# Talking-heads attention with a 64-key cut between two feed-forward blocks: sign and distance arrays awaited by their last reader only, a tie verdict in five POOL operations, value products in quarters

## The chip, the cores and the metric

The kernel runs on one core of one Trainium2 chip. Its engines are PE (TensorE, matrix products), DVE (VectorE), ACT (ScalarE), POOL (GpSimd) and SP (SyncE, which issues the DMA transfers). The metric is the device time of one launch in microseconds, the median of several runs. The profile and the trace come from one further, profiled execution.

## The reference

Input `x` is 4 batches of 1024 tokens with 256 features, all in float32. Two half-weight feed-forward blocks with ternary weights stand around an attention, each behind a layer norm:

```python
x = x + 0.5 * ffn(_layernorm(x))
x = x + attn(_layernorm(x))
x = x + 0.5 * ffn(_layernorm(x))
```

The attention has 16 heads of width 64 and 4 memory keys ahead of the 1024 keys. What sets the work around the change is this part:

```python
dots = jnp.einsum('bhid,bhjd->bhij', l2norm(q), l2norm(k)) * 10.0
dots = jnp.einsum('hg,bgij->bhij', W_pre_th, dots)
dots = jnp.where(causal, mask_value, dots)
vk = jax.lax.top_k(dots, 64)[0][..., -1:]
dots = jnp.where(dots < vk, mask_value, dots)
attn = jnp.einsum('hg,bgij->bhij', W_post_th, softmax(dots))
out = jnp.einsum('bhij,bhjd->bhid', attn, v)
```

Then `out` is scaled by head, multiplied by a sigmoid gate and projected by `Wo`.

## The kernel before

It has three parts. `first_stage` does the first feed-forward block and the projections to queries, keys, values and gates, which it stores in HBM. `attention` does the attention. `last_stage` does the second feed-forward block. The change lies in `attention` alone.

**Tiles.** A *block* is 128 tokens of a batch (`G`, 32 of them; `ib = G % 8` is its place in the batch). A block has 16 *groups* `g` of 8 tokens; with the 16 heads a group is a tile of 128 rows (head and token) by as many keys as the last token sees, 4 + 8·(t + 1) of them, so rows grow from 12 to 1028 within a batch. Two groups are a *pair* `p`, and the loop of every engine runs over pairs: `for k in range(S + 16)` with `S = 256`. In iteration `k` each engine works at several pairs at once, in stages. The order on each engine is written out by hand; engines meet by semaphores only.

**Life of a pair.** PE's `units` multiply queries and keys for the *next* block (L873, L874) into two banks, DVE's `scored` copies them to `Sn` (L1197), SP stores them (L787) and loads them back by group as `Sg` (L797). `mix` (L887) mixes heads; DVE's `take` (L1208) writes the result to `D`. The mixed scores are negated, so the cut keeps the smallest. The 64th is found by search: ACT's `count(g, r)` (L1002) counts signs against a guess `nt`, rounds `r` 0 to 3, and POOL's `better` (L1086, L1087, L1090) makes the next guess. Round 3 leaves the signs as the int8 array `SG`. POOL's `nearest` computes the count that is off (`off`), its sign (`sgn`), and the array of scaled distances `W` (L1103), and `pos`. DVE's `sides` (L1223, semaphore `near`) joins `SG` and `W`; `closest` (L1231, `best`) takes the 8 largest, `m8`; `picked` (L1239, `pick`) picks the one at place `pos`, and L1243 (`vk`) turns it into the threshold. POOL's `judge` (L1110 to L1116) writes `bad`, which is not zero where the 64th was not among the eight or where there is a tie; PE's `missed` (L900, L901) adds `bad` up inside `mix`, DVE copies the sum to `flag` (L1204) and branches on it in `threshold`. `select` (L1287, `prob`) cuts the exponentials `E`, `inverse` (L1294) inverts their sums, POOL's `spread` (L1122) scales the second mixing matrix, PE's `post` (L914) mixes, and ACT's `turned` (L1025, L1030) copies the result to `AT`.

**Value products.** When half a block (`hb`, 64 of them, one every 4 iterations) is in `AT`, PE's `values(hb, part_)` multiplies it with `V` (L934, L940) for 8 pairs of heads. Half of the pairs are done in iteration `k = 4 hb + 8`, behind `units(G, slots[1])`, and half at the start of the next iteration. The first part waits for `AT`, and in an even half also for `V` (`v_in`), which SP's `late` loads in iteration 7 of 8 (L804, L805). At the end the semaphore `av` lets DVE's `gated` (L1300) and ACT's next `turned` go on. `units` come in four `slots` per iteration, in the first six iterations of a block; each `units` call waits for DVE's copy of the one before (`s_sb`).

**POOL's order in iteration k:** `better(k-2, 3)`, `judge(k-3)`, `better(k-1, 1)`, `nearest(k-2)`, `better(k-1, 2)`, `spread` twice, `first(k)`. A `chain` around an operation makes the next one wait for it.

Of the kernel before, what the change touches and what calls it, by code (L numbers as in the profile page):

```python
# [11 lines left out]
P = 128  # L12
# [24 lines left out]
ALU = mybir.AluOpType  # L37
# [570 lines left out]
NB = B * IB  # L608
# [61 lines left out]
def attention(nc, banks, mkT, qd, kd, gd, vd, x1d, x2d, sd, mix_rows, mem_v, Wo_d, delta_c,  # L670
# [34 lines left out]
    with ExitStack() as ctx:  # L705
        def sb(name, shape, dt=F32):
            return ctx.enter_context(nc.sbuf_tensor(name, shape, dt))
# [42 lines left out]
        pick = sb("pick", [P, 8])  # L750
        vk = sb("vk", [P, 8])
        tie = sb("tie", [P, 4, 8])
        far = sb("far", [P, 8])
        bad = sb("bad", [P, 8], BF16)
        onesb = sb("onesb", [P, 1], BF16)
        deltab = sb("deltab", [R8, P], BF16)
# [105 lines left out]
        def _(pe):  # L862
# [55 lines left out]
            def values(hb, part_):  # L918
                G, ib = hb // 2, hb // 2 % IB
                if part_ == 0:  # L920
                    pe.wait_ge(s["at"], PC[8 * (hb + 1)])
                    if hb == 0:
                        pe.wait_ge(s["w_in"], 32)
                    if hb % 2 == 0:
                        pe.wait_ge(s["v_in"][G % 2], 32 * (G // 2 + 1))
                        if G >= 1:
                            pe.wait_ge(s["x_ok"], G)
                    if hb >= 1:
                        pe.wait_ge(s["ut"], hb)
                for p in range(4 * part_, 4 * part_ + 4):  # L930
                    for c in range(ib + 1):
                        for h in (2 * p, 2 * p + 1):
                            lo = DH * (h % 2)
                            out = nc.tensor.matmul(ps[7][lo:lo + DH, p * DH:(p + 1) * DH],  # L934
                                                   V[:, c, h * DH:(h + 1) * DH], AT[:, c, h, :], start=(c == 0),
                                                   stop=(c == ib and (ib > 0 or hb % 2 == 0)))
                        if c == 0 and hb % 2 == 1:
                            for h in (2 * p, 2 * p + 1):
                                lo = DH * (h % 2)
                                out = nc.tensor.matmul(ps[7][lo:lo + DH, (p + 1) * DH - R8:(p + 1) * DH],  # L940
                                                       V[0:MEM, ib + 1, h * DH:(h + 1) * DH], ATt[:, h, :],
                                                       start=False, stop=(ib == 0))
                if part_ == 1:
                    out.then_inc(s["av"], 1)

            def project(G):
# [9 lines left out]
            for k in range(S + 16):  # L956
                G = k // 8 + 1
                held = (k - 5) % 4 == 0
                slots = [range(0)] * 4
                if G < NB and k % 8 < UNITS // 4:  # L960
                    slots = unit_slots(G)[4 * (k % 8):4 * (k % 8) + 4]
                if k >= 9 and (k - 9) % 4 == 0 and (k - 9) // 4 < 2 * NB:
                    values((k - 9) // 4, 1)
                if k < S:
                    mix(2 * k, k - 3)
                if 0 <= k - 5 < S and not held:
                    post(2 * (k - 5) + 1)
                units(G, slots[0])
                if 0 <= k - 5 < S and held:
                    post(2 * (k - 5) + 1)  # L970
                if k < S:
                    mix(2 * k + 1, k - 3)
                elif searched(k - 3):
                    if k == S:
                        pe.wait_ge(s["taken"], TC[NT])
                    else:
                        pe.wait_ge(s["flag"], FP[k - 3])
                    missed(k - 3, ps[2]).then_inc(s["mixed"], 1)
                units(G, slots[1])
                if k >= 8 and (k - 8) % 4 == 0 and (k - 8) // 4 < 2 * NB:  # L980
                    values((k - 8) // 4, 0)
                if k >= 14 and (k - 14) % 8 == 0 and (k - 14) // 8 < NB:
                    project((k - 14) // 8)
                units(G, slots[2])
                if 0 <= k - 4 < S:
                    post(2 * (k - 4))
                units(G, slots[3])

        @block.scalar
        def _(act):  # L990
            def count(g, r):
                e, n, i = g % 8, reach(g), 2 * FP[g // 2] + g % 2
                act.wait_ge(s[f"nt{r}"], FP[g // 2] + 1)
                if r == 3:
                    if i >= 2:
                        act.wait_ge(s["pick"], i - 1)
                    out = SG[:, g % 2, 0:n]
                else:
                    if r == 0 and i >= 2:
                        act.wait_ge(s["cnt2"], i - 1)  # L1000
                    out = junk[:, g % 2, 0:n]
                nc.scalar.activation(out, D[:, e, 1:1 + n], ACT.Sign, bias=nt[:, r, e:e + 1], scale=-1.0,  # L1002
                                     accum_out=cnt[:, r, e:e + 1]).then_inc(s[f"cnt{r}"], 1)
# [57 lines left out]
        def _(pool):  # L1061
            links = [0]

            def chain(ins):
                links[0] += 1
                ins.then_inc(s["chain"], 1)
                pool.wait_ge(s["chain"], links[0])
# [24 lines left out]
            def nearest(p):  # L1092
                e, t = cells(p)
                pool.wait_ge(s["cnt3"], 2 * FP[p] + 2)
                chain(tt(off[:, e], tab[:, XN, t], cnt[:, 3, e], ALU.subtract))
                ts(sgn[:, e], off[:, e], -1.0, 1.0, ALU.max, ALU.min).then_inc(s["side"], 1)
                pool.wait_ge(s["side"], FP[p] + 1)
                pool.wait_ge(s["prob"], 2 * p - 2)
                for g in (2 * p, 2 * p + 1):
                    n, i = reach(g), 2 * FP[p] + g % 2  # L1100
                    if i >= 2:
                        pool.wait_ge(s["pick"], i - 1)
                    ts(W[:, g % 2, 0:n], D[:, g % 8, 1:1 + n], sgn[:, g % 8:g % 8 + 1], -SMALL, ALU.mult,  # L1103
                       ALU.mult).then_inc(s["v"], 1)
                tt(pos[:, e], off[:, e], sgn[:, e], ALU.mult).then_inc(s["pos"], 1)

            def judge(p):
                e, t = cells(p)
                pool.wait_ge(s["pos"], FP[p] + 1)
                chain(tt(tie[:, 0, e], nt[:, 3, e], sgn[:, e], ALU.mult))  # L1110
                chain(ts(tie[:, 1, e], tie[:, 0, e], SMALL, None, ALU.mult))
                ts(far[:, e], pos[:, e], 15.5, None, ALU.is_gt)
                pool.wait_ge(s["pick"], 2 * FP[p] + 2)
                chain(tt(tie[:, 2, e], m8[:, e, 0], tie[:, 1, e], ALU.add))
                chain(ts(tie[:, 3, e], tie[:, 2, e], 0.0, None, ALU.is_equal))
                tt(bad[:, e], tie[:, 3, e], far[:, e], ALU.add).then_inc(s["bad"], 1)  # L1116

            def spread(g):
                pool.wait_ge(s["rinv"], g // 2 + 1)
# [535 lines left out]
```

## Time and profile before

| | |
|---|---|
| median of 3 runs | 3963.88 us (3955.75 to 3964.03) |
| profiled execution | 3937.97 us, span on the core 3936.2 us |
| mean granted TensorE clock | 0.925 |
| PE busy | 3343.1 us (85%) |
| DVE busy | 2941.1 us (75%) |
| ACT busy | 2526.4 us (64%) |
| POOL busy | 2040.2 us (52%) |
| DMA | 466.45 MB, mean 119 GB/s |

Busy time of PE counts matmuls whose ends are modelled, so a busy PE is not one at its peak. A granted clock of 1.00 is 2.4 GHz, of 0.50 it is 1.2 GHz. The attention runs from about 996 to 3640 us of the span; the shares above average it with the two feed-forward parts. The idle time of an engine that nobody waits for costs nothing.

### The profile page before, as it was taken

The page shows a single profiled execution, that of the slowest core. Times are in us where ns is not written, and L with a number is a line of the kernel's source. Part 1 is how long each engine was busy: PE and PEld are TensorE (multiplying, and loading weights), DVE is VectorE, ACT ScalarE, POOL GpSimd, SP SyncE. Part 2 cuts the span into 40 slices and gives each one's busy share as a digit, 9 for nine tenths or more (in the row PEclk, how much of TensorE's full clock was granted, in tenths as well). Part 3 has the DMA queues.
Part 4 walks back from the last instruction along what each step waited for, and adds up shares of the span by engine and source line. Part 5 has one row for each costly group of instructions (what it writes and reads, how often), then busy time and mean ns, then how long its engine had stood idle before and what let it go on. Part 6 is the DMA issues. An engine that isn't in the chain of part 4 may idle for free. (4 is left out here: it accounts for less than half of the span.)

```text
span 3936.2 us, 72868 instructions
## 1 busy us (share of the span) xinstructions
PE 3343.1 (85%) x22950; PEld 2129.3 (54%) x22950; DVE 2941.1 (75%) x6619; ACT 2526.4 (64%) x5825; POOL 2040.2 (52%) x5777
## 2 busy tenths in 40 slices
PE   7999999995788888878888857888888888888798
PEld 4444444442455556645555644555566555566566
DVE  6778887775578888668888876888885788877254
ACT  2433443332587889768888936788895788888221
POOL 1221111222676667577666727766675776666232
PEclk9999999997699999989999977999998899999899
DMA  3222222223455654345555414555643455642110
GB/s 127 81 81 80 96 86 80 79 82 124 126 157 158 171 162 120 80 135 168 164 167 161 97 41 137 160 162 168 172 95 95 140 160 167 173 124 52 53 33 27
DMA packets 362423, 466.45 MB, mean 119 GB/s; under 512 B 29525, under 2 KB 294101, under 8 KB 361561
## 3 DMA queue, kind: packets, MB, share of 16 engines
q1 hardware_dynamic: 361944, 461.02, 40.0%
q8 instruction: 185, 3.03, 0.4%
q14 instruction: 294, 2.40, 0.2%
HBM read 226.57 MB, written 234.36 MB: 117 GB/s over the span
## 5 line engine op out<-in xcount | busy, mean ns | idle before, releaser
L1002 ACT ACTIVATE junk<-D,nt 128x76 int8<-128x76 f32 (+62 forms) x1440 | 1070.5, 746 | 178.6 <-POOL nt L1087 142.9
L914 PE MATMUL banks<-kr,E 128*128 128x128 f32 (+1 forms) x4672 | 732.4, 307 | 194.1 <-issue 96.2
L914 PEld LDWEIGHTS banks<-kr,E 128*128 128x128 f32 (+1 forms) x4672 | 627.4, 210 | 302.6 <-issue 279.1
L887 PE MATMUL banks<-Sg,kpre 128*128 128x109 f32 (+51 forms) x1568 | 647.1, 513 | 19.5 <-DVE D L1208 9.4
L873 PE MATMUL banks<-kT,qT 64*128 64x343 f32 (+11 forms) x896 | 399.6, 529 | 184.7 <-DVE Sn L1197 163.3
L1025 ACT ACTIVATE AT<-banks 128x512 f32<-128x512 f32 (+3 forms) x768 | 344.9, 478 | 324.0 <-PE banks L934 166.6
L1287 DVE SCALAR_TENSOR_TENSOR E<-D,vk,E 128x12 f32<-128x12 f32 (+56 forms) x512 | 378.4, 757 | 212.3 <-DVE vk L1243 136.0
L1223 DVE SCALAR_TENSOR_TENSOR W<-SG,sgn,W 128x76 f32<-128x76 int8 (+14 forms) x480 | 413.3, 900 | 82.9 <-POOL W L1103 80.7
L1197 DVE COPY Sn<-banks 128x686 f32<-128x686 f32 (+7 forms) x448 | 376.7, 841 | 129.9 <-PE banks L874 116.6
L523 DVE RECIPROCAL a_share<-a_share 128x512 f32<-128x512 f32 x128 | 429.2, 3353 | 4.4
L934 PE MATMUL banks<-AT,V 128*64 128x64 f32 x9216 | 367.4, 232 | 59.6 <-issue 43.4
L1002 ACT ACTIVATE SG<-D,nt 128x76 int8<-128x76 f32 (+14 forms) x480 | 356.6, 746 | 67.5 <-DVE hit L1239 65.0
L1103 POOL TENSOR_SCALAR W<-D,sgn 128x76 f32<-128x76 f32 (+14 forms) x480 | 343.2, 725 | 109.4 <-issue 72.7
L874 PE MATMUL banks<-kT,qT 64*128 64x343 f32 (+11 forms) x896 | 399.8, 529 | 0.0
L1208 DVE TENSOR_SCALAR_CACHE_REDUCE D<-banks 128x13 f32<-128x13 f32 (+62 forms) x504 | 340.1, 675 | 55.2 <-PE banks L891 54.6
L934 PEld LDWEIGHTS banks<-AT,V 128*64 128x64 f32 x9216 | 314.1, 143 | 115.1 <-issue 91.6
L1086 POOL TENSOR_TENSOR move<-cnt,tab 128x2 f32<-128x2 f32 x720 | 257.1, 357 | 210.1 <-ACT junk L1002 206.8
L887 PEld LDWEIGHTS banks<-Sg,kpre 128*128 128x128 f32 x1568 | 275.6, 210 | 149.0 <-issue 109.8
L1012 ACT ACTIVATE E<-D,least 128x12 f32<-128x12 f32 (+56 forms) x512 | 343.6, 720 | 18.3 <-DVE D L1208 16.0
L467 POOL TENSOR_TENSOR a_g2T<-a_gT 128x512 f32<-128x512 f32 x64 | 72.4, 1135 | 542.7 <-ACT a_gT L385 542.6
L1231 DVE MAX8 m<-W 128x8 f32<-128x76 f32 (+14 forms) x480 | 324.5, 712 | 0.0
L295 PE MATMUL banks<-a_xbT,a_W 128*128 128x512 f32 x512 | 248.2, 610 | 50.0 <-DVE a_share L527 49.1
(187 smaller groups left out, 5537.3 us busy)
## 6 DMA issues: line engine op xcount, KB each, us to landing
score_scratch<-Sn SPq DMA_DIRECT2D x96, 343.0 KB, 3.3
q_scratch<-a_share SPq DMA_DIRECT2D x32, 512.0 KB, 2.7
v_scratch<-a_share SPq DMA_DIRECT2D x32, 512.0 KB, 3.7
k_scratch<-a_share SPq DMA_DIRECT2D x32, 512.0 KB, 2.8
gate_scratch<-a_share SPq DMA_DIRECT2D x32, 512.0 KB, 2.8
kT<-k_scratch SPq DMA_DIRECT2D x32, 512.0 KB, 4.7
qT<-q_scratch SPq DMA_DIRECT2D x32, 512.0 KB, 6.3
gateT<-gate_scratch SPq DMA_DIRECT2D x32, 512.0 KB, 11.8
```

What stands on the lines that cost most here:

```text
L523: link(nc.vector.reciprocal(ri[:, c % 2, :], rr[:, c % 2, :]))
L873: nc.tensor.matmul(ps[0][:, 0:c1 - c0], qT[0:DH, p, :], kT[0:DH, p, c0:c1], start=True, stop=True)
L874: nc.tensor.matmul(ps[1][:, 0:c1 - c0], qT[DH:P, p, :], kT[DH:P, p, c0:c1], start=True, stop=True).then_inc(s["s_ps"], 1)
L887: out = nc.tensor.matmul(bank[:, 0:c], kpre[:].rearrange("p h r -> p (h r)"), Sg[:, g % 3, c0:c1], start=True, stop=not diagonal)
L914: out = nc.tensor.matmul(ps[5 + i % 2][0:rows, c % 4 * P:(c % 4 + 1) * P], E[:, g % 4, c * P:c * P + rows], kr[:, g % 4, :], start=True, s ...
L934: out = nc.tensor.matmul(ps[7][lo:lo + DH, p * DH:(p + 1) * DH], V[:, c, h * DH:(h + 1) * DH], AT[:, c, h, :], start=(c == 0), stop=(c == ...
L1002: nc.scalar.activation(out, D[:, e, 1:1 + n], ACT.Sign, bias=nt[:, r, e:e + 1], scale=-1.0, accum_out=cnt[:, r, e:e + 1]).then_inc(s[f"cnt ...
L1012: nc.scalar.activation(E[:, g % 4, 0:n], D[:, e, 1:1 + n], ACT.Exp, bias=least[:, e:e + 1], scale=-1.0).then_inc(s["exp"], 1)
L1025: out = nc.scalar.activation(AT[:, c0:c0 + c, :, t * R8:(t + 1) * R8], bank[:, 0:c * P].rearrange("p (c h r) -> p c h r", h=H, r=R8), ACT. ...
L1197: nc.vector.tensor_copy(Sn[:, i % 2, :, 0:c1 - c0], banks[:, 0:2, 0:c1 - c0]).then_inc(s["s_sb"], 1)
L1223: nc.vector.scalar_tensor_tensor(out=W[:, h, 0:n], in0=SG[:, h, 0:n], scalar=sgn[:, e:e + 1], in1=W[:, h, 0:n], op0=ALU.is_equal, op1=ALU. ...
L1287: nc.vector.scalar_tensor_tensor(out=E[:, g % 4, 0:n], in0=D[:, g % 8, 1:1 + n], scalar=vk[:, g % 8:g % 8 + 1], in1=E[:, g % 4, 0:n], op0= ...
```

## The change

ACT's third `count` waits for `near` (DVE has read `SG`) in place of `pick`. POOL's `nearest` waits for `best` (DVE has read `W`) in place of `pick`. `judge` drops the array `far`: a pick that found nothing leaves `vk` at zero, so the verdict is now whether the product of `vk` and the tie sum is zero. It has five operations, the third waits for `best`, the fourth for `vk`. `values` works in four parts of two pairs of heads: part 0 ahead of `units(G, slots[1])`, part 1 behind it, parts 2 and 3 at the start of the next iteration.

```diff
@@ attention
-        far = sb("far", [P, 8])
@@ values
-                for p in range(4 * part_, 4 * part_ + 4):
+                for p in range(2 * part_, 2 * part_ + 2):
...
-                if part_ == 1:
+                if part_ == 3:
                     out.then_inc(s["av"], 1)
@@ the loop on PE
                 if k >= 9 and (k - 9) % 4 == 0 and (k - 9) // 4 < 2 * NB:
-                    values((k - 9) // 4, 1)
+                    values((k - 9) // 4, 2)
+                    values((k - 9) // 4, 3)
...
+                if k >= 8 and (k - 8) % 4 == 0 and (k - 8) // 4 < 2 * NB:
+                    values((k - 8) // 4, 0)
                 units(G, slots[1])
                 if k >= 8 and (k - 8) % 4 == 0 and (k - 8) // 4 < 2 * NB:
-                    values((k - 8) // 4, 0)
+                    values((k - 8) // 4, 1)
@@ count
                 if r == 3:
                     if i >= 2:
-                        act.wait_ge(s["pick"], i - 1)
+                        act.wait_ge(s["near"], i - 1)
@@ nearest
                     if i >= 2:
-                        pool.wait_ge(s["pick"], i - 1)
+                        pool.wait_ge(s["best"], i - 1)
@@ judge
-                pool.wait_ge(s["pos"], FP[p] + 1)
+                pool.wait_ge(s["side"], FP[p] + 1)
                 chain(tt(tie[:, 0, e], nt[:, 3, e], sgn[:, e], ALU.mult))
                 chain(ts(tie[:, 1, e], tie[:, 0, e], SMALL, None, ALU.mult))
-                ts(far[:, e], pos[:, e], 15.5, None, ALU.is_gt)
-                pool.wait_ge(s["pick"], 2 * FP[p] + 2)
+                pool.wait_ge(s["best"], 2 * FP[p] + 2)
                 chain(tt(tie[:, 2, e], m8[:, e, 0], tie[:, 1, e], ALU.add))
-                chain(ts(tie[:, 3, e], tie[:, 2, e], 0.0, None, ALU.is_equal))
-                tt(bad[:, e], tie[:, 3, e], far[:, e], ALU.add).then_inc(s["bad"], 1)
+                pool.wait_ge(s["vk"], FP[p] + 1)
+                chain(tt(tie[:, 3, e], tie[:, 2, e], vk[:, e], ALU.mult))
+                ts(bad[:, e], tie[:, 3, e], 0.0, None, ALU.is_equal).then_inc(s["bad"], 1)
```

PE's order in iteration 16, where the value products of the second block begin, first before the change (each row is an instruction, its tiles and the semaphores that it waits for; lines of the changed kernel are lower by one):

```order
1100 L900 MATMUL banks<-bad,onesb 1x1 [waits t_bad0]
1101 L901 MATMUL banks<-bad,onesb 1x1
1102 L873 MATMUL banks<-kT,qT 128x258 [waits t_kmean0,t_s_sb0,t_q_in0,t_k_in1]
1103 L874 MATMUL banks<-kT,qT 128x258
1104 L934 MATMUL banks<-AT,V 64x64 [waits t_x_ok0,t_ut0,t_v_in1,t_at0]
1105 L934 MATMUL banks<-AT,V 64x64 x15
1106 L873 MATMUL banks<-kT,qT 128x259 [waits t_s_sb0]
1107 L874 MATMUL banks<-kT,qT 128x259
```

and in the changed kernel:

```order
1101 L899 MATMUL banks<-bad,onesb 1x1 [waits t_bad0]
1102 L900 MATMUL banks<-bad,onesb 1x1
1103 L933 MATMUL banks<-AT,V 64x64 [waits t_x_ok0,t_ut0,t_v_in1,t_at0]
1104 L933 MATMUL banks<-AT,V 64x64 x7
1105 L872 MATMUL banks<-kT,qT 128x258 [waits t_kmean0,t_s_sb0,t_q_in0,t_k_in1]
1106 L873 MATMUL banks<-kT,qT 128x258
1107 L933 MATMUL banks<-AT,V 64x64 x8
1108 L872 MATMUL banks<-kT,qT 128x259 [waits t_s_sb0]
1109 L873 MATMUL banks<-kT,qT 128x259
```

The score product of 128x258 has moved behind eight of the sixteen value products, and so behind their four waits. On POOL, `judge` before the change:

```order
232 L1110 TENSOR_TENSOR tie<-nt,sgn 128x2 [waits t_pos0]
233 L1111 TENSOR_SCALAR tie<-tie 128x2 [waits t_chain0]
234 L1112 TENSOR_SCALAR far<-pos 128x2 [waits t_chain0]
235 L1114 TENSOR_TENSOR tie<-m,tie 128x2 [waits t_pick0]
236 L1115 TENSOR_SCALAR tie<-tie 128x2 [waits t_chain0]
237 L1116 TENSOR_TENSOR bad<-tie,far 128x2 [waits t_chain0]
```

and in the changed kernel:

```order
226 L1112 TENSOR_TENSOR tie<-nt,sgn 128x2 [waits t_side0]
227 L1113 TENSOR_SCALAR tie<-tie 128x2 [waits t_chain0]
228 L1115 TENSOR_TENSOR tie<-m,tie 128x2 [waits t_best0,t_chain0]
229 L1117 TENSOR_TENSOR tie<-tie,vk 128x2 [waits t_vk0,t_chain0]
230 L1118 TENSOR_SCALAR bad<-tie 128x2 [waits t_chain0]
```

One instruction is gone, and two of the five wait for two semaphores.

## Rows read from the trace of the kernel before

**Rows 1.** By stretch: us, busy PE, PEld, DVE, ACT, POOL, clock, DMA share, GB/s.

```profile
996.00:3640.00 2644.00, 2221.50 (x19354) 1522.28 (x19354) 2061.48 (x5407) 2087.07 (x5143) 1774.56 (x5564) 0.91 0.50 138
```

**Rows 2.** Waits of PE, attention stage: us in total, times, longest us.

```profile
PE banks L934 <- issue: 43.4, 18, 4.3
```

**Rows 3.** Timeline, PE: start, us, engine, line, tiles, [idle before <-releaser]; an opening.

```profile
1015.50 0.98 PE L873 MATMUL banks<-kT,qT 64*128 64x389 f32 x1
...
1016.28 0.85 PE L873 MATMUL banks<-kT,qT 64*128 64x389 f32 x1
...
1021.65 1.12 PE L934 MATMUL banks<-AT,V 128*64 128x64 f32 x16 [4.48 <-DMA V<-v_scratch]
```

**Rows 4.** Timeline, PE: the opening one block later.

```profile
1073.86 0.48 PE L873 MATMUL banks<-kT,qT 64*128 64x258 f32 x1
...
1077.84 1.97 PE L934 MATMUL banks<-AT,V 128*64 128x64 f32 x32 [3.28 <-issue]
1079.74 0.80 PE L873 MATMUL banks<-kT,qT 64*128 64x259 f32 x1
...
1080.34 0.63 PE L873 MATMUL banks<-kT,qT 64*128 64x259 f32 x1
```

**Rows 5.** Timeline, PE: openings with longer rows, in the third batch.

```profile
2493.41 2.50 PE L934 MATMUL banks<-AT,V 128*64 128x64 f32 x48 [1.55 <-issue]
...
2566.68 2.08 PE L934 MATMUL banks<-AT,V 128*64 128x64 f32 x64 [2.16 <-issue]
2568.70 0.59 PE L873 MATMUL banks<-kT,qT 64*128 64x387 f32 x1
```

**Rows 6.** Timeline, DVE: copies of scores at the opening of rows 4.

```profile
1075.76 0.68 DVE L1197 COPY Sn<-banks 128x516 f32<-128x516 f32 x1
...
1081.09 0.70 DVE L1197 COPY Sn<-banks 128x518 f32<-128x518 f32 x1 [4.03 <-PE banks L874]
```

**Rows 7.** Timeline, ACT: the same opening.

```profile
1082.02 0.51 ACT L1002 ACTIVATE SG<-D,nt 128x252 int8<-128x252 f32 x1 [4.02 <-DVE hit L1239]
...
1084.08 0.38 ACT L1025 ACTIVATE AT<-banks 128x256 f32<-128x256 f32 x1 [0.96 <-PE banks L934]
```

**Rows 8.** Waits of all engines, attention stage.

```profile
ACT junk L1002 <- POOL nt L1087: 142.9, 223, 2.0
...
DVE W L1223 <- POOL W L1103: 80.7, 74, 2.2
DVE gateT L1300 <- PE banks L934: 79.7, 38, 9.8
...
ACT SG L1002 <- DVE hit L1239: 65.0, 34, 4.5
```

**Rows 9.** Timeline, DVE: a second half of a block.

```profile
2608.36 0.95 DVE L1197 COPY Sn<-banks 128x774 f32<-128x774 f32 x1
...
2616.75 0.69 DVE L1300 TENSOR_TENSOR gateT<-banks,gateT 128x512 f32<-128x512 f32 x1 [1.53 <-PE banks L934]
```

**Rows 10.** Busy time by stretch: iteration of rows 9, then behind the waits of rows 4 and 5.

```profile
2606.70:2616.70 10.00, 10.00 (x181) 7.94 (x179) 6.97 (x19) 4.27 (x12) 5.24 (x19) 1.00 0.39 126
1077.90:1084.00 6.10, 6.10 (x73) 4.98 (x73) 2.13 (x11) 1.20 (x6) 1.73 (x8) 0.50 0.28 82
2566.70:2572.00 5.30, 5.30 (x122) 4.56 (x124) 2.62 (x9) 2.75 (x9) 1.74 (x9) 1.00 0.34 118
```

**Rows 11.** Timeline, POOL: judge and nearest in an iteration of short rows.

```profile
2402.49 0.23 POOL L1111 TENSOR_SCALAR tie<-tie 128x2 f32<-128x2 f32 x1
2402.80 0.22 POOL L1112 TENSOR_SCALAR far<-pos 128x2 f32<-128x2 f32 x1
2403.08 0.22 POOL L1114 TENSOR_TENSOR tie<-m,tie 128x2 f32<-128x2 f32 x1
...
2404.81 0.23 POOL L1096 TENSOR_SCALAR sgn<-off 128x2 f32<-128x2 f32 x1
2405.14 0.83 POOL L1103 TENSOR_SCALAR W<-D,sgn 128x188 f32<-128x188 f32 x2
```

## The prediction

> **What bounds the kernel now.** I read the busy time by stage first, then the list of waits, then single stretches of the timeline. In the attention stage [rows 1] no engine is saturated: PE is busy 2221.50 of 2644.00 us, ACT 2087.07, DVE 2061.48, POOL 1774.56. The stage is bounded by whichever chain ends last in each of its 256 iterations, so each edit has to be priced where it stands.
>
> The edits touch two kinds of place. The first is the iteration in which a block's value products begin: every eighth one, called here an *opening*. The attention part has 32. The list of PE's waits [rows 2] shows that value products (L934) wait 43.4 us in 18 places for something the trace does not name. What it is shows in the one place beside these that has a name, in [rows 3]: PE has finished the score product of `units(G, slots[1])` (L873, from 1015.50, ends 1017.1) and then stands 4.48 us, until 1021.65, for the DMA into `V`. [rows 4] show the same picture one block on, now labelled "issue": the score product is done at 1074.6, the value products start at 1077.84 after 3.28 us. The second opening of [rows 5] waits 1.55 us, the third 2.16. Everybody else stands too: DVE's next copy of scores (L1197) has waited 4.03 us for PE [rows 6], ACT's `count(...,3)` 4.02 us for DVE's pick [rows 7]. So whatever PE does *after* `V` has landed is the critical path of all engines, and what it does *before* is free.
>
> The second place is POOL's `judge`, six small operations once per pair, ahead of `better(k-1, 1)`, for which ACT waits (L1087: 142.9 us in 223 places), and ahead of `nearest`, for which DVE waits (L1103: 80.7 us in 74 places) [rows 8].
>
> **Value products in quarters.** Nothing is added or removed; `units(G, slots[1])`, its copy on DVE and its store on SP go behind the first quarter. At the second opening of a batch the two lists of PE's order show this: the L934 row with the wait for `t_v_in` stood behind the two rows of 128x258, and stands ahead of them now. PE is in order, so the wait for `V` now holds the score product as well.
>
> Cost at an opening that waits. The score product was hidden in the wait; now it lies behind it. In [rows 3] it takes 1.6 us (two rounds, 0.98 and 0.85, starting 0.78 apart). In [rows 4] it ran at 0.48 us a matmul before the wait; behind the wait the clock is lower, and its twin there (128x259) takes 0.80 and 0.63, in all 1.23 us from 1079.74 to 1080.97. I take 1.2. Behind the wait of 2.16 us the twin's matmul takes 0.59 us against 0.80 [rows 5], so all of it 1.23 × 0.59 / 0.80 = 0.9 us; I take that, and for the opening of 1.55 us, which lies between, 1.1. Then `units(G, slots[2])` waits for the copy of `slots[1]`, which now runs beside the second quarter only: a copy of 0.68 us [rows 6] beside 1.0 us of products fits; with the longer rows the copy is near 1.0 us (0.95 in [rows 9]) and the quarter, half of 2.08 us [rows 5], just equals it, so I add 0.1 us. Four batches give 4 × 1.6 = 6.4, 4 × 1.2 = 4.8, 4 × 1.2 = 4.8 and 4 × 1.0 = 4.0 us, 20 in all. That is 16 openings; of the 16 others I take every third to wait as well, 5 × 1.0 us, since the 18 places are two more than 16 and short waits go under other names. Sum: **25 us later**. All engines stand there, so nothing hides it. Behind the moved copy stand two `MAX8`, the pick and, on SP, the store and the next load of `Sg`; they shift with PE. Bounds: 10 us (only the 18 waits, half a us each) to 34 us (every product at the low rate).
>
> Cost at the other half-blocks (iterations 4 of 8): PE is busy 10.00 of the 10.00 us from the moved score product to the end of the value products [rows 10], so the order of its work is neutral for it. The copy on DVE that started at 2608.36 comes later by at most a quarter's products less what DVE still had to do, about 1.1 us, and DVE then stands 1.53 us before the gating product anyway [rows 9]; over the stage it stands there 79.7 us in 38 places [rows 8], 2.1 us each: 0 us. Were it gone, 20 such iterations would cost some 10 us. Nor is there a gain: the intent could only be that PE fills a gap ahead of `units(G, slots[1])`, and in [rows 4] that product has no idle time before it.
>
> The clock. After the 3.28 us wait PE's granted clock is 0.50 (1.2 GHz) over the next 6.10 us; after the one of 2.16 us it is 1.00 (2.4 GHz) [rows 10]. The waits of the 8 openings of the 1.55 and 2.16 us kind grow by the 0.8 to 0.9 us that the score product filled, to 2.4 and 3.1 us, towards the length after which the clock was low. A stretch of 6 us at half rate gives away 3 us. Bounds 0 and 8 × 3 = 24 us; nearest are the rows of 2.16 us, full rate, so I take one stretch, **3 us**.
>
> The Trainium skill, "TensorE: Matmul & The Clock Gate", section on HAM oscillation, says that a PE which repeatedly waits for a DMA falls back to the low clock at each wait, and that the cost is half of the throttled time. It speaks against this change, since the waits grow; by it all 8 stretches would turn slow, 24 us in place of my 3, and the sum would be 37. The rows agree for the long wait only [rows 10].
>
> **The verdict in five operations.** `far` goes, 240 times. From the start of `far` to the start of the next operation is 0.28 us; from the one before it to `far` 0.31 [rows 11]. Two of the remaining five now wait for two semaphores; the nearest such row is L1103, which waits for three and starts 0.33 us behind L1096, 0.02 to 0.05 above a chained one. Net 0.28 − 2 × 0.02 = 0.24 us less per pair. It counts where POOL is the chain itself. Both DVE and ACT wait for POOL in the iterations of the short rows; DVE does so in 74 places [rows 8], of which some 24 lie just ahead of an opening's wait and are swallowed by it. 50 × 0.24 = **12 us earlier**. Bounds: 0, and 223 × 0.24 = 53 us, if every wait of ACT for L1087 passed it on. I stay near the 50, since in the long rows those waits go back to DVE's pick.
>
> Where `judge` waits for DVE, `m8` is there early and the last thing is now `vk`, 0.2 us after the pick, with two operations behind it in place of three: equal within 0.1 us, 0.
>
> **Earlier releases.** ACT's `count(...,3)` waits for `near` in place of `pick`: 65.0 us in 34 places go [rows 8]. But right behind it ACT stands again, for the value products: in [rows 7] 0.96 us after the two counts. ACT would reach that wait 4 us earlier and leave it at the same time. POOL's `nearest` waits for `best`, but `judge`, ahead of it on the same engine, waits for more. Both 0 us; bounds 0 and, if ACT's two counts of some 0.5 us were the chain in all 34, 34 us earlier.
>
> **Sum** against the profiled execution of 3937.97 us: +25 + 3 − 12 = +16 us, so 3954. The median of the runs is 3963.88, 26 us above that execution, and the measured time will be of that kind: 3964 + 16 = **3980 us**.
>
> **Rivals.**
> (a) *POOL is the bound and the change wins.* Each pair is one lap from `cnt` through `better`, `judge`, `nearest` back to `cnt`; a lap shorter by 0.24 us shortens the stage wherever ACT waits for L1087. For it: 223 such places. Against: in the openings everything stands for `V`, and in long rows POOL itself waits for DVE's pick. Price: −53 + 25 = −28 us, 3936. It decides from about 117 of the 223 laps on (28 / 0.24). Chance 0.15.
> (b) *The two edits balance.* Half of the moved score product is regained because engines that stood longer at an opening find their buffers free later. +13 − 12 = about +1, 3965. For it: PE waits 2 to 3 us again in the two iterations that follow each opening. Against: those waits are for DVE, which is late by the same amount. Chance 0.25.
> (c) *The clock rule holds in full*: 25 + 24 − 12 = +37, 4001. Chance 0.10; the row at 2.16 us is against it.
> (d) *The reordering is hidden*: the wait for `V` shrinks because its DMA is issued no later while the engines arrive later. Against: the load is issued in the iteration before, ahead of anything moved. It falls under (b).
> My forecast has 0.50.
>
> **How the numbers follow.** Unmistakable is a difference of over 0.2%, 8 us, about what a measurement of this kernel tells from none. Slower: most of the forecast (0.46), of (b) 0.02, and (c) 0.10: 0.58. Same: 0.04 of the forecast, 0.17 of (b), 0.02 of (a): 0.23. Faster: 0.13 of (a) and 0.06 of (b): 0.19. The range leaves out the far end of (a) and the top of (c): −12 to +36 us, 3952 to 4000. The forecast alone would be 3970 to 3992.
>
> **What would show it.** In the changed profile the wait of L933 at the openings must be longer by 0.7 to 1.6 us, its sum near 60 instead of 43.4, with DVE's and ACT's standing as long; the score product of 128x258 must stand behind it. The idle time before ACT's SG must be near zero and that before AT larger by as much. `judge` must take 1.37 us in place of 1.61 from first to last start. The iterations of the short rows between two openings must be shorter by 0.2 us each. I am wrong if an opening, from the last product before `V` to the next `mix`, is not longer by a microsecond, or if the iterations in between win more than 0.3 us each.

## The result, and the profile after

The changed kernel takes 4000.52 us (median of 6 runs, 3989.25 to 4008.64), the kernel before 3958.76 us on the same chip (6 runs, 3951.72 to 3964.03). The ratio is 1.010 with a 95% interval of 1.008 to 1.0121: **42 us slower**. The sign of the prediction held (3980 us); the result lies half a microsecond above the top of its range (3952 to 4000), and the size did not hold: +42 in place of +16.

The profiled executions differ by more than the medians: 4008.64 us after (the slowest of its six) and 3937.97 before (below all six). Sums over the two traces therefore overstate the loss by some two thirds, and I read them for places rather than for sizes.

The attention stage of the changed kernel, in the columns of [rows 1]:

```profile
996.00:3712.00 2716.00, 2270.66 (x19362) 1549.76 (x19363) 2062.95 (x5397) 2084.00 (x5141) 1716.68 (x5320) 0.89 0.48 134
```

All of the difference lies here, 72 us; the stages ahead of and behind it keep their lengths. DVE and ACT are busy as long as before, POOL 58 us less (the verdict's operation is gone), PE 49 us more with 8 instructions more recorded, at a granted clock of 0.89 in place of 0.91: the same matmuls, slower.

Waits of the changed kernel, attention stage (us in total, times, longest), of PE, ACT, DVE and POOL, to be held against [rows 2] and [rows 8]:

```profile
PE banks L933 <- issue: 70.1, 20, 6.7
PE banks L933 <- DMA V<-v_scratch: 13.0, 2, 7.0
...
ACT AT L1027 <- PE banks L933: 298.1, 59, 9.0
ACT junk L1004 <- POOL nt L1089: 130.9, 193, 2.1
ACT SG L1004 <- POOL nt L1089: 2.4, 4, 0.6
...
DVE Sn L1199 <- PE banks L873: 187.0, 130, 7.2
DVE gateT L1302 <- PE banks L933: 72.1, 35, 9.7
DVE W L1225 <- POOL W L1105: 72.1, 69, 2.1
```

The value products' wait is up from 43.4 to 70.1 us (with the openings in which the trace names the DMA, from 47.9 to 83.1), and DVE's wait for score products from 105.2 to 187.0. ACT no longer waits for the pick (65.0 us then, 2.4 from another source now), and stands for the value products instead: 298.1 us, where the kernel before has 166.6. The two lines of the kernel before:

```profile
DVE Sn L1197 <- PE banks L874: 105.2, 90, 4.5
```

```profile
ACT AT L1025 <- PE banks L934: 166.6, 55, 9.0
```

One opening shows what a microsecond of order turned into. It is the second of [rows 5], at iteration k = 160, where the value products of the fourth block of the third batch begin. PE in the changed kernel:

```profile
2606.74 1.98 PE L933 MATMUL banks<-AT,V 128*64 128x64 f32 x32 [3.45 <-issue]
...
2608.65 1.01 PE L873 MATMUL banks<-kT,qT 64*128 64x386 f32 x1
...
2609.46 0.85 PE L873 MATMUL banks<-kT,qT 64*128 64x386 f32 x1
2610.23 1.97 PE L933 MATMUL banks<-AT,V 128*64 128x64 f32 x32
...
2612.14 0.64 PE L873 MATMUL banks<-kT,qT 64*128 64x387 f32 x1
...
2616.14 1.18 PE L886 MATMUL banks<-Sg,kpre 128*128 128x271 f32 x4
```

and the granted clock there (columns as in [rows 1]):

```profile
2606.70:2612.00 5.30, 5.26 (x68) 4.10 (x68) 1.58 (x3) 2.30 (x8) 0.38 (x2) 0.50 0.10 31
```

In the kernel before, the mix that follows that opening starts at

```profile
2572.65 1.18 PE L887 MATMUL banks<-Sg,kpre 128*128 128x271 f32 x4
```

From the first value product to that mix the kernel before took 2572.65 − 2566.68 = 5.97 us, all of it at 2.4 GHz [rows 10]; the changed one takes 2616.14 − 2606.74 = 9.40. The score product that has moved behind the wait is 0.85 us of the 3.43 (its twin in [rows 5] takes that, from 2568.70 to the next operation at 2569.55). The rest is the clock: the wait is 3.45 us where it was 2.16, PE's clock behind it is 0.50, and what would take 2.02 + 0.85 = 2.87 us lasts from 2606.74 to 2612.14, 5.40 us: 2.5 us more.

One pair of executions cannot say, though, that the change made the clock fall at this opening. `judge_only` below has the old order of PE, and in its profiled execution the same opening went like this:

```profile
2572.28 3.68 PE L933 MATMUL banks<-AT,V 128*64 128x64 f32 x64 [2.72 <-issue]
...
2580.94 1.18 PE L886 MATMUL banks<-Sg,kpre 128*128 128x271 f32 x4
```

with this clock behind the wait (columns as in [rows 1]):

```profile
2572.30:2577.60 5.30, 5.30 (x69) 4.10 (x69) 0.40 (x1) 0.99 (x4) 0.66 (x4) 0.50 0.28 97
```

2580.94 − 2572.28 = 8.66 us with the old order at the low clock, 9.40 with the new one: 0.74 us for the order, and 2.7 us for a low clock that comes with either order. What can be counted is how often it comes. I took the granted clock of the 6 us behind the first value product of each of the 32 openings, in one profiled execution per kernel. Below 0.80 it is in 11, 13, 15, 12 and 12 openings with the old order there (the kernel before, `q_undone`, `judge_only`, `rel_only`, `ahead_odd`) and in 20, 20, 22, 17 and 24 with the new one (the changed kernel, `q_only`, `ahead_open`, `q_rel`, `q_judge`): eight more on average.

### The profile page after: what moved, and what is told of

It is laid out like the page before. It is cut to its first block and busy times, and to the rows that moved or that the text cites. A ratio compares the mean times of both kernels' runs of the same rounds, so it can differ in the third digit from the quotient of the medians.

```text
span 4006.9 us, 73108 instructions
## 1 busy us (share of the span) xinstructions
PE 3391.1 (85%) x22950; PEld 2155.8 (54%) x22950; DVE 2943.9 (73%) x6619; ACT 2523.5 (63%) x5825; POOL 1983.0 (49%) x5537
## 5 line engine op out<-in xcount | busy, mean ns | idle before, releaser
L913 PE MATMUL banks<-kr,E 128*128 128x128 f32 (+1 forms) x4672 | 741.2, 309 | 185.2 <-issue 86.9
L1027 ACT ACTIVATE AT<-banks 128x512 f32<-128x512 f32 (+3 forms) x768 | 346.3, 480 | 473.5 <-PE banks L933 298.1
L872 PE MATMUL banks<-kT,qT 64*128 64x343 f32 (+11 forms) x896 | 421.2, 554 | 177.9 <-DVE Sn L1199 156.1
L933 PE MATMUL banks<-AT,V 128*64 128x64 f32 x9216 | 387.9, 236 | 99.0 <-issue 70.1
L873 PE MATMUL banks<-kT,qT 64*128 64x343 f32 (+11 forms) x896 | 421.2, 554 | 0.0
L933 PEld LDWEIGHTS banks<-AT,V 128*64 128x64 f32 x9216 | 326.6, 146 | 162.5 <-issue 135.2
```

Source lines behind the costliest of these rows:

```text
L872: nc.tensor.matmul(ps[0][:, 0:c1 - c0], qT[0:DH, p, :], kT[0:DH, p, c0:c1], start=True, stop=True)
L873: nc.tensor.matmul(ps[1][:, 0:c1 - c0], qT[DH:P, p, :], kT[DH:P, p, c0:c1], start=True, stop=True).then_inc(s["s_ps"], 1)
L913: out = nc.tensor.matmul(ps[5 + i % 2][0:rows, c % 4 * P:(c % 4 + 1) * P], E[:, g % 4, c * P:c * P + rows], kr[:, g % 4, :], start=True, s ...
L1027: out = nc.scalar.activation(AT[:, c0:c0 + c, :, t * R8:(t + 1) * R8], bank[:, 0:c * P].rearrange("p (c h r) -> p c h r", h=H, r=R8), ACT. ...
```

## The experiments

There were twelve runs in three groups, with the quarters, the verdict and the releases taken apart first. Each ratio is against the kernel before on the same chip; 0.001 is 4 us.

**Each part alone.** `q_only` is the kernel before with the quarters and no other edit; shown is the new order, the new size of a part is left out:

```diff
+                if k >= 8 and (k - 8) % 4 == 0 and (k - 8) // 4 < 2 * NB:
+                    values((k - 8) // 4, 0)
                 units(G, slots[1])
                 if k >= 8 and (k - 8) % 4 == 0 and (k - 8) // 4 < 2 * NB:
-                    values((k - 8) // 4, 0)
+                    values((k - 8) // 4, 1)
```

> The kernel before with the quarters alone; verdict and releases as before. Theory A (the score product behind the wait for V, plus the low clock that follows, is the whole loss): slower than before by 45 to 60 us, a little more than the change itself (42 us), since the shorter verdict is missing. Theory B (the loss comes from the new waits in the verdict or the releases): within 10 us of before.

`q_undone` is the changed kernel with this edit taken back, so the verdict and the releases together.

> The changed kernel with the value products in halves as before, so verdict in five operations and earlier releases alone. Theory A: 5 to 12 us faster than before (0.24 us in some 30 to 50 laps of POOL). Theory B: slower than before by 20 us or more. If the shorter lap is swallowed by the wait for V: within 3 us of before.

`judge_only` has only the new `judge`, `rel_only` only the two lines `act.wait_ge(s["near"], i - 1)` and `pool.wait_ge(s["best"], i - 1)`.

> The kernel before with the verdict in five operations alone. All of the gain of the two small edits should be here: 5 to 12 us faster than before. If waiting for vk instead of pick costs something in the iterations in which DVE is late, 0 to 5 us slower.

> The kernel before with the earlier releases alone (near for the signs, best for the distances). My reading: no change, within 4 us of before, with ACT's wait for the pick (65 us) gone and its wait for the value products longer by as much. Rival: ACT's two counts were the chain, then 10 to 34 us faster.

| kernel | median us | ratio | 95% |
|---|---|---|---|
| q_only | 4017.02 | 1.0177 | 1.0159 to 1.0194 |
| q_undone | 3950.40 | 0.9997 | 0.9983 to 1.0012 |
| judge_only | 3953.73 | 1.0011 | 0.9997 to 1.0025 |
| rel_only | 3950.89 | 0.9997 | 0.9984 to 1.0009 |

The whole loss is the quarters'. Alone they cost 1.77%, 70 us (65 by the difference of the medians), more than the change as a whole. The verdict and the releases are worth nothing that these runs can tell without the quarters. The verdict's missing gain is seen in the wait for `V`. PE in `judge_only`:

```profile
PE banks L933 <- issue: 53.9, 19, 5.1
```

and in `q_undone`:

```profile
PE banks L933 <- issue: 56.0, 19, 4.9
```

against the 43.4 of [rows 2]. The iterations ahead of an opening do get shorter by 0.27 us each, in some 18 places (from one `rinv` of DVE to the next, in both traces), 5 us in all, and PE then stands longer at the openings: 53.9 and 56.0 us in place of 47.9 (43.4, and the 4.48 of [rows 3]).

That these waits are for `V`, though the trace calls them "issue", can be read off SP. From its second transfer into `V` (L805) to the first value product it takes, as means of the first five blocks of a batch, 10.2 to 10.9 us in the kernel before, 10.3 to 11.3 in `q_undone` and 10.3 to 11.1 in the changed kernel, whatever PE does meanwhile.

**Which half-blocks.** Both kernels are the changed one, with the first quarter ahead of `units(G, slots[1])` in only some iterations: for `ahead_open` in iterations 0 of 8, the openings, for `ahead_odd` in iterations 4 of 8.

```diff
+                due = k >= 8 and (k - 8) % 4 == 0 and (k - 8) // 4 < 2 * NB
+                ahead = k % 8 == 4
+                if due and ahead:
+                    values((k - 8) // 4, 0)
                 units(G, slots[1])
+                if due and not ahead:
+                    values((k - 8) // 4, 0)
+                if due:
+                    values((k - 8) // 4, 1)
```

> The changed kernel, but the first quarter goes ahead of the score product only in the openings (iteration 0 of 8, where the wait for V stands); in iteration 4 of 8 both quarters come behind it. If only the openings cost: as slow as the change, 38 to 45 us over before. If iteration 4 costs too (its period grew by 0.6 to 1.4 us in the profile): 25 to 35 us over before.

> The complement: the first quarter ahead of the score product only in iteration 4 of 8, where PE had no gap. If only the openings cost: 5 to 10 us faster than before, like the kernel without quarters. If iteration 4 costs too: 5 to 15 us slower than that one.

`ahead_open` 3996.86 us, ratio 1.0106 (1.008 to 1.0132); `ahead_odd` 3954.35 us, 1.0002 (0.9986 to 1.0018). The loss comes from the 32 openings alone; behind a block's middle the same reordering is free, to within 7 us. Nor do all openings pay: in the sixth and seventh block PE does not wait for `V`, and in six of these eight openings the iteration is at most 0.15 us longer (15.65 and 15.21 us in `ahead_open`, from one pair of `bad` products to the next, in place of 15.51 and 15.06 in `q_undone`); the other two are longer by 0.7 to 0.8.

**How much of it is the clock.** `warm_after` keeps the changed order and gives PE products of 128x128 to do, into the bank that the value products overwrite, before it waits for `V`:

```diff
+                    if hb % 2 == 0 and hb >= 2:
+                        for _ in range(WARM.get(ib, 0)):
+                            nc.tensor.matmul(ps[7][:, 0:P], ...)
```

with `WARM = {0: 18, 1: 16, 2: 8, 3: 8, 4: 6}` by block of the batch.

> The changed kernel with 6 to 18 idle products of a constant into the bank of the value products ahead of the wait for V, in the openings of the first five blocks of a batch. They read and write nothing that is used. If the low clock behind the longer wait is more than half of the loss: 20 to 35 us faster than the change, and the score product behind the wait takes 0.7 to 1.0 us instead of 1.2 to 1.9. If the loss is the order alone: within 5 us of the change.

3986.52 us, ratio 1.0085 (1.0062 to 1.0108). That is 35 us over the kernel before on the same chip, where the changed kernel is 42 over and `ahead_open` 45: a gain of 6 to 10 us, with intervals that overlap, and below what I expected. (The 14 us between this median and the changed kernel's 4000.52 are no measure: the kernel before is 7 us faster, too, beside the one than beside the other.) PE at the opening of [rows 4] in this kernel (L927 are the fillers, each recorded as two):

```profile
1075.99 4.55 PE L927 MATMUL banks<-kpre 128*128 128x128 f32 x32
1080.57 0.69 PE L938 MATMUL banks<-AT,V 128*64 128x64 f32 x16
1081.18 0.48 PE L873 MATMUL banks<-kT,qT 64*128 64x258 f32 x1
```

The quarter takes 0.69 us here. In the changed kernel it takes 1.12, behind a wait of 6.66 us:

```profile
1081.28 1.12 PE L933 MATMUL banks<-AT,V 128*64 128x64 f32 x16 [6.66 <-issue]
1082.33 0.79 PE L872 MATMUL banks<-kT,qT 64*128 64x258 f32 x1
```

So the clock is kept here, and 35 us of the loss remain. It is kept at most openings, not at all: the low clock comes in 7 of the 32, among them three of the third blocks, where PE waits another 1.83 to 3.91 us behind too few fillers and then reads 0.72 or 0.73. A second reading agrees in size. Over the 29 runs of the kernel before that stand beside the first group, a mean granted clock lower by 0.001 goes with 2.1 us more. Its mean clock there is 0.9197, that of the changed kernel's six runs, taken at another time, 0.9152: 4.5 × 2.1 = 9 us. A third is an estimate of what it can be at most: 6 us times one less the clock, summed over the 32 openings, is 24 to 32 us in the five kernels with the old order and 39 to 57 in the five with the new one, 19 us more on average, if all of it lies on the path. The clock thus accounts for 6 to 19 us of 42; where in between is not shown.

**The other way round: an earlier load.** If what stands behind `V`'s landing is the path, an earlier landing should win. `early_v` is the kernel before with the two transfers into `V` issued at k % 8 == 6, ahead of the next block's keys and queries, and taken out of `late`:

```diff
+                if k % 8 == 6 and G < NB:
+                    fetch(G)
                 if k % 8 == 6 and G + 2 < NB:
                     keys(G + 2)
                     queries(G + 2)
```

> The kernel before with the load of V issued one iteration earlier (6 of 8), ahead of the keys and queries of the next block but one. If the openings are bound by that load: the waits of the value products in the openings of the first five blocks go (about 45 us of idle time), and the kernel is 30 to 60 us faster than before. If something else is late next (the pick, the probabilities): 0 to 15 us faster.

3999.61 us, ratio 1.0121 (1.0094 to 1.0149): **48 us slower**, where 30 to 60 us faster were expected. The wait for `V` is gone from PE's list, and this has come in its place:

```profile
PE banks L892 <- DMA Sg<-score_scratch: 77.4, 23, 6.0
```

Issues of this kernel, KB each, median us to landing:

```profile
kT<-k_scratch SPq DMA_DIRECT2D x32, 512.0 KB, 12.2
qT<-q_scratch SPq DMA_DIRECT2D x32, 512.0 KB, 14.1
```

and of the kernel before:

```profile
kT<-k_scratch SPq DMA_DIRECT2D x32, 512.0 KB, 4.7
qT<-q_scratch SPq DMA_DIRECT2D x32, 512.0 KB, 6.3
```

Three transfers of some 500 KB now run together, and the `Sg` load that SP issues behind them, which the next `mix` needs, comes late. The Trainium skill, "DMA: Bandwidth & Descriptors", section "Queues, rings and completion order", says that on each DMA engine a queue's descriptors are taken in ring order; these rows agree with it: what is issued behind `V` on SP pays for `V`. Transfers that only share the bandwidth would look the same, and SP itself is held up, too: it spends 7.04 us on issuing the `Sg` load at 1068.40. Which of these it is was not tested. The load's place in the kernel before was the better one of the two.

**Verdict and releases on top of the quarters.** The quarters alone cost 70 us, the whole change 42. Which of the other two gives back the difference? `q_rel` is `q_only` with the releases, `q_judge` is `q_only` with the verdict.

> The kernel before with the quarters and the two earlier releases (near, best), and the old verdict on POOL. Quarters alone were +65 to 70 us against before, all three edits +42; so the other two give back about 25 us once the quarters are in, although each was worth 0 alone. Theory one (the releases do it: with the quarters DVE's pick comes late behind the wait for V, and ACT's SG count and POOL's nearest, which waited for the pick, stood in the chain): this kernel comes out near +42 to +48. Rival (the shorter verdict does it, since POOL's laps are the chain in the delayed iterations behind an opening): this kernel stays near +65 to +70. Half each: near +55.

> The kernel before with the quarters and the new five-operation verdict, which waits for vk and side, and the old releases. The theory that the releases alone give back the 25 us expects +63 to +70 against before; the rival, that the shorter verdict does, expects +42 to +48; half each: near +55. Outside the first stage of each iteration nothing else differs from the run with the quarters alone.

`q_rel` 4008.74 us, ratio 1.0148 (1.0121 to 1.0174); `q_judge` 4012.22 us, 1.0146 (1.0123 to 1.0169). Against 1.0177 each gives back some 12 us; neither theory of "it alone" holds, and half each, the third case, does. The intervals overlap that of `q_only`, which ran on another chip, so 12 is a best value and no more. Where the releases get it shows in ACT's waits. `q_only`:

```profile
ACT AT L1028 <- PE banks L934: 142.5, 53, 9.0
ACT SG L1005 <- DVE hit L1242: 141.6, 47, 6.4
```

`q_rel`:

```profile
ACT AT L1028 <- PE banks L934: 275.1, 59, 9.0
...
ACT SG L1005 <- POOL nt L1090: 2.3, 4, 0.6
```

With the quarters DVE's two `MAX8` and the pick stand behind the copy of a score product that itself waits for `V`, and ACT's wait for the pick more than doubles, from 65.0 us [rows 8] to 141.6. The releases take it away; 132.6 us of it come back as a wait for the value products. That the rest, 6.7 us, is the gain is a guess of the right size.

**Further in the opposite direction.** If one score product behind the wait costs, one more ahead of it should win. `fill_open` is `q_undone` with `units(G, slots[2])`, too, ahead of the value products at the openings:

```diff
                 units(G, slots[1])
+                if k % 8 == 0:
+                    units(G, slots[2])
                 if k >= 8 and (k - 8) % 4 == 0 and (k - 8) // 4 < 2 * NB:
                     values((k - 8) // 4, 0)
```

> The verdict and the releases with the value products in halves, and the order at the openings (iterations 0 of 8) turned the other way: the next score product too, units(G, slots[2]), goes ahead of the first half's wait for V. Theory (what stands behind V's landing is the chain of all engines, what stands ahead is free, and a shorter wait keeps the clock up): the mirror of the change, 16 waits shorter by 1.0 to 1.3 us, so 15 to 35 us faster than before. Rival (V lands a constant time after its issue, the wait is not the bound but the order of work behind it: the copies of scores on DVE now bunch up ahead of V and post(2(k-4)) waits as it did, or ATs wait for the values longer): within 5 us of before. It would be slower only if the store of scores and the Sg load behind it were delayed, which this order makes earlier.

3961.36 us, ratio 1.002 (1.0007 to 1.0032): 8 us **slower**. The expectation fell. PE's waits in it:

```profile
PE banks L872 <- DVE Sn L1199: 189.0, 124, 36.3
...
PE banks L933 <- issue: 20.9, 9, 4.7
```

and in `q_undone`:

```profile
PE banks L872 <- DVE Sn L1196: 145.2, 94, 36.3
```

The wait ahead of the value products is shorter by 35 us as expected (56.0 to 20.9), and the wait for DVE's copy of scores is longer by 44. The opening at k = 48, the sixth block of a batch, shows why; PE, then DVE:

```profile
1402.60 0.94 PE L872 MATMUL banks<-kT,qT 64*128 64x343 f32 x1 [1.88 <-DVE Sn L1199]
...
1404.04 3.70 PE L933 MATMUL banks<-AT,V 128*64 128x64 f32 x96
```

```profile
1398.90 1.91 DVE L1225 SCALAR_TENSOR_TENSOR W<-SG,sgn,W 128x748 f32<-128x748 int8 x2
...
1401.69 0.86 DVE L1199 COPY Sn<-banks 128x686 f32<-128x686 f32 x1
```

In `q_undone` PE does not wait at this place at all. The next score product needs the bank that DVE empties at 1401.69 to 1402.55, behind its passes over the long rows; PE, which would have had 3.0 us of value products to do meanwhile, stands for 1.88 us, and its matmuls then take 0.94 us in place of 0.55. Over the eight iterations from an opening on, the mean of four batches is shorter by 1.2 and 1.6 us in the first and third block, and longer by 2.2 and 3.9 in the fifth and sixth, and by 4.0 in the second, for which I have no cause. An order that fills only the first blocks' waits was not tried.

**The same with fillers.** `fill_warm` adds 16, 12 and 6 fillers in the first three blocks of a batch to `fill_open`.

> The same order as fill_open, and ahead of the wait for V at the first three openings of each batch 16, 12 and 6 products of 128x128 into the free bank ps[7], whose results are overwritten. In the changed kernel such products gave back 14 of 42 us. If the low clock behind V's wait costs the kernel before as well (the 6 us at 0.50 in the rows read before), this kernel is 5 to 15 us faster than fill_open, its mean granted clock above it; if the clock matters only where the waits grew, or the fillers reach past V's landing, it is within 3 us of fill_open or slower.

3995.10 us, ratio 1.0109 (1.0083 to 1.0135), worse than `fill_open` by 0.9%. The fillers were mis-sized, as the opening of [rows 4] shows in this kernel:

```profile
1074.79 4.66 PE L927 MATMUL banks<-kpre 128*128 128x128 f32 x24
1079.38 1.15 PE L938 MATMUL banks<-AT,V 128*64 128x64 f32 x32
```

They run for 4.66 us, where `fill_open` has only 0.94 us of waiting left. The value products are at full rate (1.15 us; 1.97 in `fill_open`), but they start 8.5 us behind the opening's first score product (1070.85 to 1079.38), in `fill_open` 5.1 us (1073.79 to 1078.88). From SP's second transfer into `V` to the first value product it takes 13.9 and 13.1 us in the second and third block, where `fill_open` takes 10.7 and 10.9: the fillers reach past `V`'s landing. What the clock alone would have given does not show in this run. In `warm_after` the same distance is 10.6 to 11.0 us in the first five blocks, so there they do not.

## Why the prediction was right in sign and wrong in size

**What bounds the kernel.** Right. "Whatever PE does after `V` has landed is the critical path of all engines" fits `ahead_open` (+42 us) and `ahead_odd` (0), and the distance from SP's transfer to the first value product, which hardly moves. "What it does before is free" is right for what stood there, and wrong as a rule: `fill_open` puts more there and pays.

**Value products in quarters, +25 and +3.** Measured +65 to +70 for the quarters alone. This is the term that was mis-sized, in at least two places.

- *The clock, 3 us.* Measured 6 to 19 us in the whole change, and by the slope above (0.9197 − 0.9120) / 0.001 × 2.1 = 16 in `q_only`. The step that failed is "nearest are the rows of 2.16 us, full rate, so I take one stretch": the traces count eight more low stretches where I took one. The row told of one wait in one execution. At that very opening the clock was 0.50 behind 3.45 us in the changed kernel, but also behind 2.72 us in `judge_only` with the old order, and 1.00 behind 1.60 us in `q_undone`. The other kind, of 1.55 us, I had put with the full-rate ones without asking its clock, and in the kernel before it reads 0.72:

```profile
2493.40:2499.40 6.00, 5.99 (x102) 4.89 (x104) 1.81 (x8) 2.16 (x8) 1.60 (x9) 0.72 0.23 78
```

  Rival (c), by the rule of the Trainium skill's "TensorE: Matmul & The Clock Gate", section on HAM oscillation, said that all these stretches would turn slow, +37 us and 4001. That section speaks of waits that outlast the clock gate's window, a condition that the prediction left out. Of the rivals and the forecast (c) came nearest in number and in the count of stretches; its price of 3 us for each, 24 in all, is above the 6 to 19 measured, and its −12 for the verdict alone did not come. I had given it 0.10.
- *The order, 25 us.* What the clock leaves of the 42 is 23 to 36 us. That holds the forecast's 25, but no run has the order alone, so it doesn't prove it. It is not a microsecond for each opening: where PE does not wait for `V` it is mostly 0.14.
- *What stands behind the moved copy.* "Two `MAX8`, the pick and the store shift with PE" was said and priced at nothing beyond PE's own delay. ACT's wait for the pick grew by 77 us in `q_only`. By difference this would cost the rest of the quarters' 65 to 70 us less the clock's 16 and the forecast's 25 for the order, 24 to 29, of which 12 came back with the releases. None of these parts was measured by itself; how the sum divides stays open.

**The other half-blocks, 0.** Right, by `ahead_odd`.

**The verdict, −12.** Alone it gives nothing (+4 us, −1 to +10). Its working was right on the lap: from the first to the last start of `judge` it is now 1.16 us, where it was 1.47 in a lap that waits for nothing (POOL; the changed kernel):

```profile
2885.73 0.20 POOL L1112 TENSOR_TENSOR tie<-nt,sgn 128x2 f32<-128x2 f32 x1
...
2886.89 0.22 POOL L1118 TENSOR_SCALAR bad<-tie 128x2 bf16<-128x2 f32 x1
```

and the kernel before:

```profile
2845.37 0.21 POOL L1110 TENSOR_TENSOR tie<-nt,sgn 128x2 f32<-128x2 f32 x1
...
2846.84 0.19 POOL L1116 TENSOR_TENSOR bad<-tie,far 128x2 bf16<-128x2 f32 x1
```

Wrong were the 50 laps: some 18 iterations are shorter, by 0.27 us, and most of them stand just ahead of an opening, whose wait takes the gain. I had left out 24 of 74 for this reason and should have left out all. With the quarters in it was worth some 12 us, the number forecast; where it gets them there no run shows, so this proves none of the working.

**The releases, 0.** Right alone (`rel_only` 0.9997), wrong beside the quarters, some 12 us. The argument, "ACT would reach that wait 4 us earlier and leave it at the same time", was read in the old order, in which the pick came 1 us ahead of the value products' end.

**The sum.** That the forecast came within 26 us of the loss has luck in it: the quarters were put 37 to 42 us too low, and some 12 us each came back from two edits that give nothing without them.

**The signs.** The value products' wait near 60 us: 70.1. ACT's idle time ahead of SG near zero: 2.4. That ahead of AT larger by as much, 65 us: larger by 131; `q_undone`, without the quarters, has 251.1 us, 85 more than before, so the rest is the value products' coming later. `judge` shorter by 0.24 us: by 0.31. An opening longer by a microsecond: 3.43 us in the one shown, 0.74 of them against an execution of the old order at the same clock.

**Rivals (a) and (b).** (a) needed 117 laps and there are 18. (b) held that half of the score product is regained behind the opening; at the one shown 0.74 to 0.85 us, nearly all of it, is still there at the next mix, and the 42 us leave little room for it.

## What to carry over

An operation that fills an engine's wait for a transfer costs nothing where it stands. Moved behind the wait it costs its whole time, and here also the clock of what follows in more places: the wait grows, and its *new* length has to be asked, in more than one execution. A gain ahead of a wait with a fixed end was worth nothing, and so was a gap filled with work whose buffer another engine had yet to empty. Edits that are worth nothing alone may be worth something beside a third, so take a change apart in both surroundings before a part is dropped.

## What I had not expected of the hardware

- The length of a wait does not settle the clock behind it. In `q_undone` (k = 216) one of 3.40 us is followed by 6 us at 2.4 GHz, in `q_only` (k = 128) one of 1.62 us by 6 us at 1.2 GHz. First value product and stretch (columns as in [rows 1]), `q_undone`, then `q_only`:

```profile
3161.91 1.62 PE L933 MATMUL banks<-AT,V 128*64 128x64 f32 x48 [3.40 <-issue]
```

```profile
3161.90:3167.90 6.00, 5.99 (x111) 4.69 (x113) 2.73 (x12) 2.20 (x8) 1.72 (x7) 1.00 0.35 99
```

```profile
2295.80 3.68 PE L934 MATMUL banks<-AT,V 128*64 128x64 f32 x64 [1.62 <-ACT AT L1028]
```

```profile
2295.80:2301.80 6.00, 6.00 (x92) 5.22 (x94) 3.02 (x7) 4.35 (x6) 3.96 (x11) 0.51 0.01 3
```

  The same place can go either way in kernels with the same order of PE: at k = 160 the clock is 1.00 in the kernel before and in `q_undone`, 0.50 in `judge_only`. So it has to be counted over many openings and kernels.

- Runs of one kernel differ in mean granted clock (0.915 to 0.926 in `rel_only`), and their time follows it at about 2 us per 0.001.
- With 496 KB put ahead of them on SP's queue, two loads took 12.2 and 14.1 us to landing in place of 4.7 and 6.3, and the kernel lost 48 us by a load that was only issued earlier.
